# A two-layer gated cross-attention and expert kernel: another order of loads, clearings and writes ahead of layer 0, and Newton steps moved to the normalisation

## The reference

```python
def _layernorm(x, axis=-1, eps=1e-05):
    return (x - mean(x)) / sqrt(var(x) + eps)
...
# layer 0 attention
logits = einsum('bhqd,bhkd->bhqk', q, k) / sqrt(dh)
logits = logits + ((1.0 - mask) * -1000000000.0)[:, None, :, :]
attn = softmax(logits) * group_prob[:, None, :, :]
return (attn @ v) @ wo_k + wo_b
...
x = x + tanh(g_xattn[0]) * _L0_xattn_ref(_layernorm(x), ctx_1024, ctx_1024, fside_BxSxS2_0, mask_BxSxS2_ik1, ...)
x = x + tanh(g_ffn[0])   * _L0_ffn_ref(_layernorm(x), ...)    # top-2 experts with a capacity, gelu
x = x + tanh(g_xattn[1]) * _L1_xattn_ref(_layernorm(x), ctx_1024, ctx_1024, mask_1x1xSxS2_bk1, ...)
x = x + tanh(g_ffn[1])   * _L1_ffn_ref(_layernorm(x), ...)    # top-2 of 8 gated experts, all computed
return x
```

## Time and profile before

| what | value |
|---|---|
| median of 3 runs | 950.13 us (949.31 to 952.72) |
| the profiled execution, its own time | 948.68 us |
| its span | 946.9 us |
| busy PE, DVE, ACT, POOL | 83%, 73%, 64%, 58% |
| granted TensorE clock, mean | 0.946 of full speed |
| DMA | 101.7 MB, mean 107 GB/s |
| layer 0 slots, experts, layer 1 slots begin (first maxima, first job, first maxima) | 34.2, 318, 449.6 us |

### The profile page before, as it was taken

How to read it: one execution, slowest core, us unless ns; L and a number is a source line. 1 busy time by engine, 2 the same in 40 slices (tenths; PEclk the granted TensorE clock), 3 DMA queues, 4 the chain that set the end, 5 groups by cost and what they waited for, 6 DMA issues and landing times.

```text
span 946.9 us, 20428 instructions
## 1 busy us (share of the span) xinstructions
PE 786.9 (83%) x6554; PEld 621.2 (66%) x6554; DVE 689.9 (73%) x1980; ACT 610.0 (64%) x2582; POOL 547.0 (58%) x798
## 2 busy tenths in 40 slices
PE   3658989989866599999767778689888889999996
PEld 1446766667644499998455556467666668888885
DVE  5748899999968334454878898888897675666654
ACT  2648988889853355443866777789996544444442
POOL 4254578888675202030747775863423967777775
PEclk9879999999977799999978998999998999999998
DMA  7969886766337443224427257446300000000000
GB/s 186 215 189 259 212 260 159 169 148 140 75 76 256 146 146 90 75 83 110 97 57 151 73 112 157 111 122 125 96 13 24 23 23 23 24 23 12 1 11 23
DMA packets 85139, 101.68 MB, mean 107 GB/s; under 512 B 8448, under 2 KB 70853, under 8 KB 84360
## 3 DMA queue, kind: packets, MB, share of 16 engines
q1 hardware_dynamic: 80936, 92.13, 38.0%
q0 software_dynamic: 4096, 8.25, 3.5%
HBM read 63.32 MB, written 45.99 MB: 115 GB/s over the span
## 4 chain that ended last, share of the span: by engine, by line
PE 38%; DVE 23%; ACT 12%; POOL 10%; issue 10%; DMA 5%; SPq 1%; POOLq 0%; DVEq 0%; ACTq 0%
ACT exp L854 10%; PE psum L697 7%; PE psum L737 5%; DVE shift L1039 5%; PE psum L739 5%; PE psum L738 5%; DVE exp_T L1049 2%; DVE ln_stats L1021 2%; POOL got_rows L1587 2%; PE psum L685 2%; DVE exp_T L1051 2%; PE psum L686 2%; PE psum L687 2%; PE psum L580 2%; DMA scratch_q<-parts 2%
## 5 line engine op out<-in xcount | busy, mean ns | idle before, releaser
L854 ACT ACTIVATE exp<-psum,shift 128x120 f32<-128x120 f32 x1024 | 366.7, 437 | 86.2 <-DVE shift L1039 85.7
L854 ACT ACTIVATION_READ_ACCUMULATOR exp<-psum,shift 128x1 f32 x1024 | 273.4, 282 | 0.0
L567 PE MATMUL psum<-ident,exp 128*120 128x128 f32 x1024 | 166.3, 287 | 50.4 <-DVE exp_T L1051 31.0
L1039 DVE TENSOR_REDUCE shift<-psum 128x4 f32<-128x480 f32 x256 | 165.6, 648 | 34.8 <-PE psum L558 33.4
L567 PEld LDWEIGHTS psum<-ident,exp 128*120 128x120 f32 x1024 | 120.2, 143 | 71.0 <-DVE exp_T L1051 37.5
L1422 DVE SCALAR_TENSOR_TENSOR q_operand<-psum,comb,q_operand 128x256 f32<-128x256 f32 x256 | 111.5, 479 | 72.3 <-ACT q_operand L986 72.3
L1659 POOL TENSOR_TENSOR q_operand<-q_operand 128x512 f32<-128x512 f32 x96 | 126.4, 1316 | 58.2 <-DVE q_operand L1422 53.4
L986 ACT ACTIVATE q_operand<-psum 128x512 f32<-128x512 f32 x128 | 76.3, 599 | 113.7 <-PE psum L739 113.7
L1587 POOL DMA_INDIRECT got_rows<-scratch_y,slot_get x64 | 67.1, 1049 | 122.8 <-DMA scratch_y<-y_rows 106.5
L555 PE MATMUL psum<-neg_rows,const_bf 128*128 128x480 bf16 x256 | 98.4, 385 | 36.7 <-ACT exp L854 28.5
L558 PE MATMUL psum<-k_operand,q_operand 128*128 128x240 bf16 x512 | 97.6, 273 | 0.0
(11 more groups left out here) (175 smaller groups left out, 1672.5 us busy)
## 6 DMA issues: line engine op xcount, KB each, us to landing
k_operand<-scratch_k SPq DMA_DIRECT2D x32, 360.0 KB, 6.4
q_operand<-scratch_q SPq DMA_DIRECT2D x30, 384.0 KB, 6.1
scratch_q<-parts SPq DMA_DIRECT2D x15, 384.0 KB, 2.5
scratch_k<-parts SPq DMA_DIRECT2D x14, 360.0 KB, 4.9
scratch_xe<-in_zero_rows SPq DMA_DIRECT2D x8, 512.0 KB, 7.3
scratch_y<-in_zero_rows SPq DMA_DIRECT2D x8, 512.0 KB, 7.4
scratch_q<-parts SPq DMA_DIRECT2D x15, 256.0 KB, 2.3
scratch_k<-parts SPq DMA_DIRECT2D x14, 240.0 KB, 4.7
```

The lines of the kernel that those rows point to most:

```text
L567: ins = pe.transpose(ps[0:S2, T_BANKS[G % 2], u * S:(u + 1) * S], atts[l].expS[:, G % RING_E, u, :], ident[:, :])
L854: ins = act.activation(atts[l].expS[:, G % RING_E, u, :], ps[:, S_BANKS[G % 3], u * S2:(u + 1) * S2], ACT.Exp, bias=atts[l].shift[:, i % 2 ...
L1039: dve.tensor_reduce(atts[l].shift[:, i % 2, 4 * r:4 * r + 4], ps[:, S_BANKS[G % 3], 0:4 * S2].rearrange("p (h k) -> p h k", h=4), AX_X, AL ...
```

## The change

Two groups of edits; no instruction is added or taken away.

In layer 0's preamble GpSimd clears ring 1 ahead of the power of chunk 1 and ring 2 right behind `masks(0)` (before, in slot 0, behind the bias additions). SP writes the first part of q ahead of `fetch_k(0)`, loads the group behind the q parts, and loads the masks of chunk 1 right behind `fetch_q(0)` (before, in slot 0, behind both fetches of chunk 1). The rows of chunk 2 and the spares stand later, and `fetch_k(1)` and `fetch_q(1)` go to slot 4, behind the rows of chunk 3. Chunk 2's preparation starts in slot 4 and not 2.

The Newton step on VectorE stands directly ahead of the normalisation, two or three slots behind where it stood: for chunks 1 to 3 of layer 1, for the half of chunk 9 behind the experts, and for the second layer norm of chunks 6 and 7 of layer 0. The gathers of chunks 5, 6 and 7 start in slots 29, 37 and 52 (before 30, 45 and 60).

```diff
-    return ({1: 0, 2: 2} if l == 0 else {1: 0, 2: 0, 3: 0}).get(P, 16 * P - 38)
+    return ({1: 0, 2: 4} if l == 0 else {1: 0, 2: 0, 3: 0}).get(P, 16 * P - 38)
...
+FETCH_READY = 4
...
-    return {8: 0, 9: 7, 10: 9, 11: 11}[i] if c == 2 else {3: 13, 4: 21, 5: 30, 6: 45, 7: 60}[c] + 2 * b
+    return {8: 0, 9: 7, 10: 9, 11: 11}[i] if c == 2 else {3: 13, 4: 21, 5: 29, 6: 37, 7: 52}[c] + 2 * b
...
                 if l == 1 and P in ON_DVE1:
-                    if o == at["power"]:
+                    if o == at["norm"]:
                         roots(0, C)
-                    if o == at["norm"]:
                         normalise_rows(0, C, P)
...
-                if l == 0 and j >= ON_DVE and o == post_at(l, j)["power"]:
+                if l == 0 and j >= ON_DVE and o == post_at(l, j)["norm"]:
                     roots(1, j)
-                if l == 0 and j >= ON_DVE and o == post_at(l, j)["norm"]:
                     normalise_rows(1, j, j)
...
+                if n == NORM_NEXT:
                     roots(0, HALVED, 1)
-                if n == NORM_NEXT:
                     normalise_rows(0, HALVED, 1, 1)
...
-            if l == 0 and s == 0:
-                clear_ring(2)
...
         pool.memset(vx[:], 0.0).then_inc(spread0, 1)
+        clear_ring(1)
         powers(0, 1)
-        clear_ring(1)
         masks(0)
+        clear_ring(2)
...
-                if s == 0:
-                    load_masks(1)
...
+            if l == 0 and s == FETCH_READY:
+                fetch_k(1)
+                fetch_q(1)
...
         load_masks(0)
-        load_group(0)
         for p in range(3):
             parts_out(1, 0, p)
+        parts_out(0, 0, 0)
         fetch_k(0)
-        for p in range(3):
-            parts_out(0, 0, p)
+        parts_out(0, 0, 1)
+        parts_out(0, 0, 2)
+        load_group(0)
         fetch_q(0)
-        load_rows(2)
-        clear_spares(1, RING)
+        load_masks(1)
         for p in range(3):
             parts_out(1, 1, p)
+        load_rows(2)
         for p in range(3):
             parts_out(0, 1, p)
-        fetch_k(1)
-        fetch_q(1)
+        clear_spares(1, RING)
         attention(0)
```

## The result

The changed kernel took 928.2 us (median of 4 runs, 926.8 to 928.9) beside 950.56 us of the kernel before (4 runs on the same chip). That is 22.4 us less by the medians; the ratio is 0.976 (95% interval 0.974 to 0.978), which is 22.7 us. The prediction was 926 us, with a range from 914 to 938. The profiled execution took 927.88 us, its span 926.1 us (before 948.68 and 946.9). Measured twice more, beside the experiments, the same kernel gave ratios of 0.9776 and 0.9772.

A forecast was written before the change was run, and what follows sets the result against it. No engine was taken to bound the kernel alone (TensorE 38% of the chain); gains lay in shared waits. 11.6 + 3.8 + 4.5 + 4.0 = 23.9 us off 948.7 gives 924.8, plus 1.4 for the median: 926, range 914 to 938.

The forecast's parts named there:

- Bound and place: Whole kernel: no engine carries the chain alone, so gains come where all stand still, first at the late masks(1).
- Term 1: Start of layer 0: the earlier mask load closes the hole and the first chunk's fetch comes sooner; 11.6 us, range 5 to 13.
- 10.4 for the hole: Layer 0, slot 10: with the mask early it would start at about 49.9 in place of 60.34, 10.4 us.
- the 1.2: Before slot 0: VectorE's cast of q ends earlier, beside no clearing; 1.2 us taken, bounds 2.5 gain or 0.7 loss.
- third rival: Layer 0's preamble: clearing ring 1 blocks VectorE's normalising, 2 to 3 us of gain lost, 928.5 us; chance 0.07.
- first rival: Slots 16 to 32 of layer 0: the DMA queue becomes the bound, 2 to 6 us lost, 928 to 932; chance 0.20.
- thin cover: Layer 0, slot 32: chunk 2's fetch lands at about 85, when TensorE asks for it; costed at nothing.
- Term 2: End of layer 0: the later Newton step removes VectorE's 4.13 us wait for GpSimd's power; 3.8 us, bounds 2 and 4.1.
- Term 3: Layer 1: later Newton steps remove three VectorE stops of 1.49, 1.49 and 2.79 us; 4.5 us, range 0 to 5.8.
- I count 1.5, 1.5 and 1.5: Layer 1's three Newton stops: 1.5 us each, as GpSimd would deliver normalised rows no earlier behind the third.
- Term 4: Layer 1: earlier gathers fall into GpSimd's idle times and end VectorE's waits; 4 us, range -2 to 8.

The follow-up runs named there:

- b_roots0: The kernel before with only the Newton step of chunks 6 and 7 at the end of layer 0 moved to the normalisation; ratio 0.9970, 2.9 us less.
- b_roots1: The kernel before with only layer 1's Newton steps (chunks 1 to 3, the half behind the experts) moved to the normalisation; ratio 0.9967, 3.1 us less.
- a_spread: The changed kernel with gathers of chunks 6 and 7 spread two in three slots, from 43 and 55; ratio 0.9809 to the kernel before.
- b_mask: The kernel before with only the masks of chunk 1 loaded right behind the first fetch of q; 958.9 us, ratio 0.9925.
- b_bring: The kernel before with only the gathers of chunks 5, 6 and 7 moved to slots 29, 37 and 52; ratio 0.9950, 4.8 us less.

## Why the prediction was right, and where it was not

**Bound and place: right.** The hole at slots 9 to 12 came from the late mask; it is gone, and TensorE's wait for `v_spread` with it. The first job of the experts came 14.0 us earlier, forecast 15.4. masks(1) came at 35.4, not at 31: the fetch it stands behind was itself 1.5 us later than before, and the mask then took 6.9 us from issue to use where I had counted 6. It had 12 us of cover.

**Term 1, 11.6 forecast, 9.8 in the trace, 10.2 measured alone.** The 10.4 for the hole were too few and the 1.2 had the wrong sign. From slot 8 to slot 16 after gained 12.5 us; 1.7 were lost before slot 0, and 1.0 between slots 16 and 24, most of it at one wait of VectorE for TensorE (1.19 us, before 0.47), which I did not follow further. The failing step is "Bounds: all 2.5 us, or a loss of 0.7; I take 1.2". The third rival, which I gave 0.07, is what happened: normalising 3.0 us later, and the cast of q, which should have been free at 0.41, met the third clearing and took 2.33. The trace agrees with the Trainium skill (SBUF — State Buffer, section "Who interferes with whom") for this form, 1.11 against 4.09 us; I had held one row without the collision against it, and that row could not speak on it. The 10.4 were also credited to the mask alone. Alone it bought 6.6 us at slot 16; the traces put the rest down to the rows of chunk 3, which now stand ahead of the fetches, and to TensorE's lower clock behind the stop that they cause. That term 1 came out within 1.8 us is in part luck: 2.1 us too few for the hole and 2.9 too many for the start nearly cancel. With 2 to 3 us off for it, the third rival's time was 928.5 us, the nearest to the measured one.

**The first rival, the queue: no.** Slot 32 began at 88.45 with the lead of slot 24, 9.8 us, and its maxima wait for nothing. The thin cover held.

**Term 2, 3.8 forecast, 2.9 (1.6 to 4.1) alone.** From slot 120 to the last slots of layer 0 the trace of b_roots0 gains 4.3 us; in after the lead grew there from 9.6 to 14.3, 4.7 us. GpSimd could follow, as the earlier trace rows said.

**Term 3, 4.5 forecast, 3.1 (1.6 to 4.8) alone.** Up to slot 32 the gain was larger than forecast (7.1 us in b_roots1), then 3.4 of it were lost in slots 32 to 63. The step "I count 1.5, 1.5 and 1.5" booked a share for GpSimd at one stop; it should have asked what GpSimd does two chunks on, when VectorE arrives there 7 us earlier and, with the gathers where they were, waits for them.

**Term 4, 4.0 forecast, 4.8 (2.9 to 6.6) alone.** Nearest to the waits that the rows showed, as chosen. The price in slots 32 to 47 was put at 1 to 3 and was 2.7. My check "slots 32 to 47 in at most 38" failed at 40.3, since terms 3 and 4 both pay there: 2.5 and 2.7 us alone, 4.6 together.

The errors were -1.4, -0.9, -1.4 and +0.8 us of gain by the kernels with one part each, and the time came out 2 us above the forecast.

## What to carry to other kernels

A hole in a trace can hide waits behind it: before pricing the removal of the longest wait, look which loads are asked for next to it, since the second of them sets what is gained. Move a prefetch by where its consumer stands, not to level out the load of the engine that issues it; eight gathers in a row cost 1.4 to 2.7 us around their place, and spread out and close to their use they came late and the kernel was 3.5 us slower. When an engine idles through a clearing, check which in-order neighbour runs at that time: 3 us of memset made 1.1 us of normalising into 4.1.

## What the runs showed of the hardware

- A GpSimd memset of 3840 words per partition (3.30 us) holds VectorE's f32 `tensor_scalar` and its f32-to-bf16 cast until it ends: 1.11 to 4.09 us, 0.43 to 2.33, 3.31 and, beside two in a row, 4.97 us. A waiting cast did not get in between the two. Two `tensor_tensor` operations inside such memsets took 0.69 us, as long as elsewhere (before, 28.21; after, 19.16); one beside GpSimd's `tensor_scalar` for the mask took 0.95 (before, 20.12).
- VectorE's additions of gathered rows (`scalar_tensor_tensor`, mostly 0.34 us) were in every version some of them much longer; the longest took 3.19 us before, 1.99 after and 1.91 in a_spread, and GpSimd was at work beside each.
- After a stop TensorE came back at the lower of its two levels: in b_mask it was busy for 0.41 us from 52.3 to 56.2, and from 56.2 to 61.3 the granted clock was 0.50 and 32 weighted sums took 1.93 us instead of 1.08. Behind the 9.26 us wait of the kernel before and behind 3.57 us in a_spread they took 1.94, both at 0.50.
- Chips differ by more than the change of a part: 948.5 to 970.3 us for the same kernel before, while the ratio of after to before stayed within 0.976 to 0.978. Up to slot 80 of layer 0 the traces of two chips agree within 0.8 us (186.94 and 187.70). Windows of the experts' stretch, the kernel before and then b_bring, whose code is the same up to there, on the slower chip:

```profile
318.00:449.00 131.00, 128.51 (x943) 123.33 (x944) 58.61 (x141) 61.92 (x124) 15.68 (x17) 0.97 0.36 100
```

```profile
327.00:464.00 137.00, 129.16 (x942) 123.43 (x942) 58.47 (x141) 61.52 (x124) 16.57 (x18) 0.96 0.35 98
```

TensorE is busy for the same time and stands still for longer; what it waits for there was not followed. Kernels are best set side by side slot by slot on one chip; where I went across chips, differences under 1 us say nothing.
